# One more interleaving at the end of a layer kernel: the eighth block's dense layers on the other set of buffers, and three small matmuls stacked into one

## What is computed

```python
x = x + attention(layernorm(x))       # 8 x 512 tokens of 256 channels, sparse attention
x = x + sparse_ffn(layernorm(x))      # router keeps 4 of 16 groups of 64 hidden units
x = x + block_b(layernorm(x))         # gated linear attention, then dense layers
x = x + sparse_ffn(layernorm(x))

def block_b(x, ...):                  # x here is the normed input
    xb = swapaxes(rmsnorm(x, scale1), 0, 1)
    q, k, v = xb @ wq.T, xb @ wk.T, xb @ wv.T
    gate_hidden = silu(xb @ wg1.T + bg1)                       # 16 channels
    alpha = sigmoid((gate_hidden @ wg2.T + bg2) / 16)          # the decay, 256 channels
    # scan over 8 steps: S = alpha * S + k v^T;  o = q S
    out = headnorm(o) * silu(xb @ wog.T + bog) @ wo.T
    x = x + out
    n = rmsnorm(x, scale2)
    return x + (silu(n @ w_gate.T) * (n @ w_up.T)) @ w_down.T  # hidden size 1024
```

## Time and profile before

| | |
|---|---|
| median of 3 runs | 1687.62 us (1687.0 to 1689.92) |
| the profiled execution | 1682.62 us |
| its span, first to last instruction | 1680.9 us |
| PE / DVE / ACT / POOL busy | 1490.2 / 1111.5 / 663.6 / 550.5 us |
| mean granted PE clock | 0.947 |

### The profile page before, as it was taken

One profiled execution on the slowest core, in us unless ns is written; L12 is line 12 of the kernel. 1 busy time (PEld: TensorE's weight loads), 2 busy tenths in 40 slices (PEclk: granted clock), 3 DMA queues, 4 the chain that ended last, 5 costly groups with the idle time before them and its releaser, 6 DMA issues.

```text
span 1680.9 us, 25260 instructions
## 1 busy us (share of the span) xinstructions
PE 1490.2 (89%) x8707; PEld 1057.1 (63%) x8756; DVE 1111.5 (66%) x2182; ACT 663.6 (39%) x924; POOL 550.5 (33%) x697
## 2 busy tenths in 40 slices
PE   4688998998898559999998899999999999999888
PEld 2333443343343148888877688878788787877676
DVE  3778778777877865555656858576674857575432
ACT  1176666666666512322233333323343332322211
POOL 5345534534632012513220323223322323233130
PEclk8599899999999969999999999999999999999997
DMA  5222312222222030011100100001010100101000
...
DMA packets 56285, 60.99 MB, mean 36 GB/s; under 512 B 15637, under 2 KB 41509, under 8 KB 56221
## 3 DMA queue, kind: packets, MB, share of 16 engines
...
...
q10 hardware_dynamic: 288, 0.00, 0.0%
...
## 4 chain that ended last, share of the span: by engine, by line
PE 50%; issue 23%; DVE 12%; POOL 9%; ACT 5%; DMA 1%; POOLq 0%; DVEq 0%; another core or an unknown queue 0%; ACTq 0%; SPq 0%
PE ps L1730 12%; PE ps L1758 9%; PE ps L810 6%; PE ps L783 4%; PE ps L797 4%; PE ps L744 3%; POOL h L1358 3%; DVE mc L497 3%; PE ps L1741 2%; POOL kT L1336 2%; PE ps L752 2%; ACT pT0a L671 2%; PE ps L1770 1%; PE ps L1716 1%; DVE race L601 1%
## 5 line engine op out<-in xcount | busy, mean ns | idle before, releaser
L497 DVE TENSOR_REDUCE mc<-ps 128x2 f32<-128x1024 f32 x256 | 306.2, 1220 | 42.5 <-PE ps L783 42.3
L1758 PE MATMUL ps<-w_hi,h 128*128 128x256 f32 x1024 | 224.3, 302 | 0.3 <-DVE h L1578 0.3
L250 POOL DMA_DIRECT2D k_st<-k_hi x256 | 123.2, 487 | 259.4 <-PE ps L797 245.3
L1639 ACT ACTIVATE h<-ps 128x512 fp32r<-128x512 f32 x128 | 76.5, 598 | 328.9 <-PE ps L1791 202.9
L1730 PE MATMUL ps<-xT_b,w_hi 128*128 128x512 f32 x512 | 176.6, 427 | 5.7 <-ACT maskT L1633 5.7
L1358 POOL TENSOR_TENSOR h<-hf,h 128x512 fp32r<-128x512 f32 x64 | 82.8, 1294 | 301.9 <-DVE h L1589 301.9
L1758 PEld LDWEIGHTS ps<-w_hi,h 128*128 128x128 f32 x1024 | 168.1, 191 | 5.4 <-DVE h L1578 3.5
L1578 DVE SCALAR_TENSOR_TENSOR h<-ps,h 128x512 fp32r<-128x512 f32 x128 | 88.4, 691 | 124.1 <-ACT h L1639 122.8
L783 PE MATMUL ps<-k_st,q_st 48*128 48x512 f32 x512 | 138.4, 538 | 35.8 <-DVE mc L497 34.7
L783 PEld LDWEIGHTS ps<-k_st,q_st 48*128 48x128 f32 x512 | 52.2, 200 | 166.7 <-issue 82.0
L1758 PE MATMUL ps<-w_lo,h 128*128 128x256 f32 x512 | 143.9, 281 | 0.0
...
## 6 DMA issues: line engine op xcount, KB each, us to landing
q_st<-q_hi SPq DMA_DIRECT2D x256, 32.0 KB, 2.0
k_st<-k_hi POOLq DMA_DIRECT2D x256, 32.0 KB, 1.9
q_st<-q_lo SPq DMA_DIRECT2D x128, 32.0 KB, 2.1
k_st<-k_lo POOLq DMA_DIRECT2D x128, 32.0 KB, 1.9
...
```

Of the source, the lines that this page charges most:

```text
L250: eng.dma_start((q_st, k_st)[which][par][64 * e + DH * r:64 * e + DH * r + DH, j, :].bitcast(F32), src[(2 * j + e) * DH:(2 * j + e + 1) * ...
L497: v.tensor_reduce(mc[par][:, qt, 2 * HU + j:MC:NPAIR], ps[:, at:at + 2, :], AX_X, ALU.max).then_inc(max_done, 1)
L1639: a.activation(h[s][m % 2][0][:, :], ps[:, RING[s] + m % 2, :], ACT.Relu).then_inc(F[s]["relu"], 1)
L1758: last = t_.matmul(ps[:, ACC[s] + t // 2, (t % 2) * D:(t % 2 + 1) * D], h[s][m % 2][a][:, t * P:(t + 1) * P], ws[k][:, m, :], start=m == 0 ...
```

## The change

1. The last part of the program is a new list, `CLOSE`. Block 7's dense layers become steps `e.*` on set 0 (they also write the layer norm's input for it there), and its second sparse layer runs as `f0.*` on set 0. Both are interleaved with block 6's sparse layer (`f1.*`, set 1). `CLOSE` begins with the rest of block 7's linear part up to `o.T`, then comes block 6's dense layer with `z.y` and `o.wo` ahead of `g.d7`.
2. New steps: `e.rms`, `e.gT`, `e.m`, `e.u`, `e.d`, `e.x` (POOL adds x + y into `x[0]`), `e.gend`, `e.ln`, `e.T`, `e.rt`, `e.lg`, `e.end`. SP stores block 7 from `x[0]` when `e.end` is done.
3. The gate's 16 channels are computed three times over, at rows 0, 32 and 64, by repeated columns of `w_g1`. `gT` holds high, high and low halves there, `w_g2` high, low and high ones; so one matmul makes what three made. The raw weights and `bg1` are loaded three times, by small transfers.

```diff
-FINAL = ["g.T", "rec7", "g.m0", "g.u0", "g.m1", "o.x", "g.u1", "g.d0", "g.m2", "z.y", "g.u2", "g.d1", "g.m3",
...
+CLOSE = ["rec7", "o.mean", "o.ln", "o.T", "g.T", "g.m0", "g.u0", "g.m1", "g.u1", "g.d0", "g.m2", "g.u2",
+        "g.d1", "g.m3", "g.u3", "g.d2", "g.m4", "o.x", "g.u4", "g.d3", "g.m5", "g.u5", "g.d4", "g.m6", "g.u6", "g.d5",
+        "g.m7", "g.u7", "g.d6", "z.y", "o.wo", "g.d7", "g.end", "e.rms", "e.gT", "e.m0", "e.x", "f1.ln", "e.u0",
+        "e.m1", "f1.T", "e.u1", "f1.rt", "f1.lg", "f1.m0c", "e.d0", "e.m2", "e.u2", "f1.mk", "e.d1", "f1.m0", "e.m3",
+        "f1.m1", "e.u3", "e.d2", "f1.d0", "e.m4", "e.u4", "e.d3", "e.m5", "e.u5", "e.d4", "e.m6", "e.u6", "e.d5",
+        "e.m7", "e.u7", "e.d6", "f1.m2", "e.d7", "f1.d1", "e.gend", "e.ln", "f1.m3", "f1.d2", "f1.m4", "e.T", "f1.d3",
+        "f1.m5", "f1.d4", "e.rt", "e.lg", "f0.m0c", "f1.m6", "f1.d5", "f0.mk", "f1.m7", "f0.m0", "f0.m1", "f1.d6",
+        "f0.d0", "f0.m2", "f0.d1", "f0.m3", "f0.d2", "f0.m4", "f0.d3", "f0.m5", "f0.d4", "f0.m6", "f0.d5", "f0.m7",
+        "f0.d6", "f1.d7", "f1.end", "f0.d7", "e.end"]
...
+FINAL = [closing(name) for name in CLOSE]
...
-    hf = [[w[:, 0, :]], [sb(f"hf1{k}", [P, L], F32) for k in range(2)]]
+    hf = [[w[:, k, :] for k in range(2)], [sb(f"hf1{k}", [P, L], F32) for k in range(2)]]
...
+    thrice = [t[:, :, 0:3 * QUAD].rearrange("p c (r n) -> p c r n", n=QUAD)[:, :, :, 0:NE] for t in w_g1]
+    late.append((None, *thrice, g1_raw[:, :, :].unsqueeze(2).to_broadcast([P, NC, 3, NE])))
+    late.append((None, w_g2[:, :], w_g2[QUAD:2 * QUAD, :], g2_raw[:, :]))
...
+    for r in range(3):
+        last_loads.append((g2_raw[QUAD * r:QUAD * r + NE, :], dram["wg2"]))
+        last_loads.append((bg1[QUAD * r:QUAD * r + NE, :], dram["bg1"]))
...
-        for j in (NBLK - 2, NBLK - 1):
-            store(j)
+        store(NBLK - 2)
+        eng.wait_ge(last_out, 1)
+        for e in range(2):
+            ld(dram["out_blocks"][e, bass.ts(NBLK - 1, PB), :, :], x[0][e * PB:(e + 1) * PB, :, :], x_out)
...
+        def last_over(i):
+
+            eng.wait_ge(x_in, 32 * NBLK)
+            g.tensor_tensor(x[0][:, :, :], x[0][:, :, :], y[:, :, :], ALU.add).then_inc(LS["xy"], 1)
...
-            for t in gT:
-                last = v.memset(t[:, :].bitcast(F32), 0.0)
-            link(last)
...
+        def last_rms(i):
+            eng.wait_ge(G["rn"], NBLK)
+            rms_scaled(tok[0], y, squares[:, :]).then_inc(T[0]["src"], 1)
...
-            link(v.tensor_copy(gT[0][0:NE, :], g_in))
-            v.tensor_tensor(gT[1][0:NE, :], g_in, gT[0][0:NE, :].bitcast(F32), ALU.subtract).then_inc(Z["ghs"], 1)
+            g_in, low_rows = hf[0][0], slice(2 * QUAD, P)
+            link(v.tensor_copy(gT[:, :], g_in))
+            v.tensor_tensor(gT[low_rows, :], g_in[low_rows, :], gT[low_rows, :].bitcast(F32),
+                            ALU.subtract).then_inc(Z["ghs"], 1)
...
-            for k, (a, b) in enumerate(PASSES):
-                last = t_.matmul(ps[:, bank, :], w_g2[a][:, c * P:(c + 1) * P], gT[b][:, :],
-                                 start=k == 0, stop=k == len(PASSES) - 1)
-            last.then_inc(Z["out"], 1)
+            t_.matmul(ps[:, bank, :], w_g2[:, c * P:(c + 1) * P], gT[:, :],
+                      start=True, stop=True).then_inc(Z["out"], 1)
```

More of the change, by code:

```diff
@@ L1125, in block_part, with last_turn @@
     G = site("g", "ss", "rn", "xy", "gate", "silu", "up", "pd", "hh", "hl", "dm")
-    f1_out = sem("f1_out")
+    LS = site("last", "xy", "gate", "silu", "up", "pd", "hh", "hl", "dm")
+    f1_out, last_out = sem("f1_out"), sem("last_out")
     def turn(k, second):
         return 2 * k + second
+    def last_turn(second):
+        return turn(FIRST + NBLK, second)
     def z_turn(i, second):
@@ L1174, in late_in @@
     def late_in(n):
-        return (late_raw, 16 * NLATE) if n < NLATE else (last_raw, 16 * (len(late) - NLATE))
-    small = [(t[:, :], dram[name]) for name, t in (("bg2", bg2), ("s1", s1), ("s2", s2), ("bg1", bg1))]
+        return (late_raw, 16 * NLATE) if n < NLATE else (last_raw, 16 * len(last_loads))
+    small = [(t[:, :], dram[name]) for name, t in (("bg2", bg2), ("s1", s1), ("s2", s2))]
     small += [(bog_all[:, :], dram["bog"].partition_broadcast(P))]
@@ L1218, in sp @@
                 eng.wait_ge(pads_cleared, 1)
-                for src, _, _, raw in late[NLATE:]:
-                    ld(raw, src, last_raw)
+                for out, in_ in last_loads:
+                    ld(out, in_, last_raw)
             if n == NGROUP - 2:
@@ L1298, in late_low @@
             eng.wait_ge(late_hi, n + 1)
+            if n == len(late) - 1:
+                eng.wait_ge(late_lo, n)
+                raw, hi = g2_raw[QUAD:2 * QUAD, :], lo
             g.tensor_tensor(lo, raw, hi.bitcast(F32), ALU.subtract).then_inc(late_lo, 1)
+            if n == len(late) - 1:
+                eng.wait_ge(late_lo, n + 1)
         def pads(i):
@@ L1304, in pads @@
                 g.memset(t[:, :, :].bitcast(F32), 0.0)
-            for t in w_g2:
-                last = g.memset(t[:, :].bitcast(F32), 0.0)
-            last.then_inc(pads_cleared, 1)
+            g.memset(bg1[:, :], 0.0)
+            g.memset(g2_raw[:, :], 0.0).then_inc(pads_cleared, 1)
         def bias(k, s):
@@ L1367, in pool @@
             parts[f"p{s}.x"] = lambda k, s=s: bias(k, s)
-            parts[f"f{s}.ln"] = lambda i, s=s: ffn_ln(i, s)
+            parts[f"f{s}.ln"] = lambda i, s=s: ffn_ln(i, s, turn(i, 1))
+        parts["e.rms"] = out_rms
+        parts["e.x"] = last_over
+        parts["e.ln"] = lambda i: ffn_ln(FIRST, 0, last_turn(1))
+        for m in range(NM):
+            parts[f"e.u{m}"] = lambda j, m=m: low_h(0, 0, m, LS, "hh")
         for m in range(NM):
@@ L1608, in dve @@
             parts[f"g.u{m}"] = lambda j, m=m: gated(j, m)
+            parts[f"e.u{m}"] = lambda j, m=m: gated(0, m, 0, LS)
+        parts |= {"e.rms": last_rms, "e.gT": lambda j: low(last_turn(0), 0, s2), "e.gend": last_g_end,
+                  "e.ln": lambda k: layer_norm(FIRST, 0, tok[0], F[0], x[0]).then_inc(T[0]["src"], 1),
+                  "e.T": lambda k: low(last_turn(1), 0), "e.lg": lambda k: choose(FIRST, 0), "e.end": last_end}
         run(eng, parts, link, DVE_LINKS_B)
@@ L1655, in og_silu, with silu @@
             a.activation(og[:, :, :], og[:, :, :], ACT.Silu).then_inc(Z["ogs"], 1)
-        def silu(j, m):
-            eng.wait_ge(G["gate"], NM * j + m + 1)
+        def silu(j, m, s=1, S=G):
+            eng.wait_ge(S["gate"], NM * j + m + 1)
             if m >= 2:
-                eng.wait_ge(G["hl"], NM * j + m - 1)
-            a.activation(hf[1][m % 2][:, :], ps[:, RING[1], :], ACT.Silu).then_inc(G["silu"], 1)
+                eng.wait_ge(S["hl"], NM * j + m - 1)
+            a.activation(hf[s][m % 2][:, :], ps[:, RING[s], :], ACT.Silu).then_inc(S["silu"], 1)
         def o_squares(i):
@@ L1762, in down, with router @@
             last.then_inc(S["dm"], 1)
-        def router(i, s):
-            eng.wait_ge(T[s]["lo"], NC * (turn(i, 1) + 1))
+        def router(i, s, turns):
+            eng.wait_ge(T[s]["lo"], NC * (turns + 1))
             for t in range(NT):
@@ L1865, in pe @@
             parts[f"f{s}.T"] = lambda k, s=s: transposed(turn(k, 1), s)
[L1866 removed]
+            parts[f"f{s}.rt"] = lambda i, s=s: router(i, s, turn(i, 1))
             parts[f"f{s}.mk"] = lambda i, s=s: masks(i, s)
@@ L1879, in pe @@
             parts[f"g.d{m}"] = lambda j, m=m: down(j, 1, m, w_down, G)
+            parts[f"e.m{m}"] = lambda j, m=m: gate(0, m, 0, LS)
+            parts[f"e.u{m}"] = lambda j, m=m: up(0, m, 0, LS)
+            parts[f"e.d{m}"] = lambda j, m=m: down(0, 0, m, w_down, LS)
+        parts |= {"e.gT": lambda j: transposed(last_turn(0), 0), "e.T": lambda j: transposed(last_turn(1), 0),
+                  "e.rt": lambda j: router(FIRST, 0, last_turn(1))}
         eng.wait_ge(given["ffn_lo"], len(given["ffn_pieces"]))
```

75 lines of the change are left out of this document (43 added, 32 removed), and 4 rows, old and new, of the table FINAL.

## The result

The changed kernel takes 1679.62 us in the median of 20 runs beside 1688.38 us for the kernel before on the same chip; the ratio of the runs is 0.9962, with a 95% interval of 0.9945 to 0.9979, so 6.4 us (3.5 to 9.3) faster. The two medians alone lie 8.8 us apart; all comparisons here go by the ratio. Run twice more, on other chips, the ratio was 0.9960 (0.9933 to 0.9987) and 0.9987 (0.9965 to 1.0009). The three weighted by their intervals give 0.997, about 5 us. The forecast was -3.7 us.

The account below looks back on a forecast made before the run. The prediction took TensorE (PE) to bound the kernel, with idle and half-clock stretches after the loop. PE's end -4.1, tail +0.9 and stacking -0.5 made -3.7 us, from 1687.62 to 1683.9 us; range 1677.5 to 1690.

Parts of the forecast that it names:

- Part 1, the stacking: One matmul instead of three for z.o7 and z.o8: mostly hidden in the loop, -0.5 us in all from blocks 0 to 2.
- Rival (b): PE is late at the gate projections after all, so stacking pays in full: 7 us more, 1677 us; 6%.
- Part 2, the head: Start of CLOSE, rec7 to g.m0: PE waits 3.4 us before o.mean and 5.9 before o.T; costs 15.1 us.
- The recovery: Dense work behind g.m0 runs 4.4 us at half clock after the head's idling, losing 2.2 us.
- Part 3, the middle: Block 6's dense layer to PE's end: 5.4 us idle before e.gT, full from f1.rt; PE ends at 1670.8, against 1674.9.
- Rival (a): In the middle, POOL's x + y doesn't block DVE's small operation and scaling: 4.1 us less, 1679.8 us; 15%.
- Rival (d): In the interleaved closing, DVE serves both streams in order and delays low halves: 8 us slower, 1692 us; 12%.
- Part 4, the tail: From PE's end to the span's end: the two blocks' stores come close together, so the second ends 0.9 us later.
- Rival (c): Clock stays low longer, in head and middle (1.6 us more each) or some loop turns (1.7 each): 1687.2 us; 21%.

Follow-up runs that it names:

- after again: The changed kernel, unmodified, run and profiled a second time on another chip; ratio to the kernel before 0.9960 (0.9933 to 0.9987).
- the first arrangement: Changed kernel with the closing's head and middle reordered into block 6's dense layer and POOL's x + y held until the scaling is done; ratio to before 0.9900.

## Why the prediction was right

The working was checked in three profiles of the changed kernel. From the last mask transposes on, before takes 199.4 us, 197.9 without its dip. After takes 192.9, 194.6 and, without its dip, 194.9: so -5.0, -3.2 and -3.0. The terms of the closing that I had summed, -4.1 at PE's end and +0.9 behind it, are -3.2. The mechanism was right there. That the whole came out near -3.7 us is in part luck, since the sum left out the dips, five in each profile of before and none, two and four in those of after, at 1.56 us each. From block 0's masks to the end the three profiles of after are 9.8, 3.5 and 3.1 us under those of before. The runs' -6.4 us in one comparison and -2.2 (0.9987) in another may differ for this reason; that isn't shown, as their intervals overlap and only profiled executions show dips.

*Part 1, the stacking, -0.5 us.* It is 0 by the profiles; this term was wrong. f1.T's wait was to grow to 1.16 us; PE waits 0.45 us at z.o8 and 0.69 at f1.T, 1.14 together. I hadn't seen that z.o8 would wait for ScalarE to clear its bank, but that lies in the same hidden time. In blocks 0 to 2, where I had put 0.5 us, the stretch ahead of the first turn grew by 0.4 to 0.7 us (145.9 to 146.3 in five profiles with the stacking, 145.6 in the one without, all with the same stretches at half clock) and the first turn shrank by 0.4 (93.85 instead of 94.25 to 94.31), which nearly cancels. Rival (b) fell.

*Part 2, the head.* Waits of 3.4 and 5.9 us were forecast, 3.26 and 5.74 measured. From rec7's start to g.m0 I had 17.7 us (1531.1 less 1513.41); it is 17.4 in the first profile (1532.71 less 1515.33) and 18.0 in the other two. The recovery was a term of 2.2 us. In the first profile there was none: dense work starts at a clock of 1.00. In the other two it starts at half, and e.m0 comes 2.07 us later for it. First after, then after again, the 3.5 us behind g.m0:
```profile
1532.71:1536.20 3.49, 3.49 (x15) 2.86 (x16) 0.32 (x1) 1.06 (x2) 0.00 (x0) 1.00 0.00 0
```
```profile
1534.67:1538.20 3.53, 3.53 (x9) 2.82 (x10) 0.00 (x0) 1.03 (x2) 0.00 (x0) 0.55 0.00 0
```
So the size was right two times in three; I had made it a fixed cost, and it is one that some executions have.

*Part 3, the middle.* `ve_b` at 2.4 us: 2.23. The gap ahead of e.gT, 5.4 us: 5.16. From e.m0 to f1.rt 9.1 us: 8.97. From f1.rt to PE's end 82.8 us: 84.1 in all three profiles. Here a step failed: I counted f1.rt and what follows at full clock, and there is a second half-clock stretch (mean 0.75 over 6.81 us). It takes the 1.3 us that were missing: in the run with POOL's addition held back, where that stretch is absent, f1.rt to PE's end is 82.5 us. PE without waits from there on was right, 0.3 us in 77.3:
```profile
1587.19:1594.00 6.81, 6.81 (x37) 6.22 (x38) 3.51 (x22) 0.00 (x0) 1.28 (x1) 0.75 0.00 1
1594.00:1671.30 77.30, 76.98 (x479) 66.11 (x483) 27.38 (x68) 15.31 (x26) 11.18 (x8) 1.00 0.00 1
```
Rival (a), the free port, fell: `ve_b` was stretched. It had priced 4.1 us, 2.4 at e.gT and 1.7 at f1.rt; the addition held back gave 2.1 us at e.m0, of which 1.2 were left at f1.rt. Rival (d) fell for this order of the list and came true in another, the first arrangement.

*Part 4, the tail*, +0.9 us: PE's end to the span's end is 6.4 to 6.6 us in the three profiles, 5.9 before, so +0.5 to +0.7.

*Rival (c)* was half right. The clock does stay low longer in some executions, in the head, by 2 us. But I gave it "a turn or two of the loop" because of longer waits at f1.T, and the waits there pull nothing down: they are the same in turns with and without a dip, and the dips came fewer and not more. I took the five dips of the one profile before for a property of the kernel, since they came each time. In the changed kernel, with the same waits of 1.34 to 1.35 us ahead of the mask transposes, they come or stay away, by where the first falls. The range, 1677.5 to 1690, had room for that; the working had no term for it.

The head is where the change gives most of its gain away. PE's waits of over 0.6 us behind the last masks sum to 19.5 us in the third profile of before and to 17.3 in after, so the change fills old waits and opens nearly as many new ones; the rest of its 3 to 5 us is work no longer done at half clock. The forecast had this sum. It didn't ask whether the same steps could be listed without the new waits, and that was worth more than the change: -20 us with the head alone reordered, and -26 with the middle and the loop's order as well, instead of -5.
